# A graph network in two passes: relu rows summed in two halves of the partitions, late products of quads in pass 1

## The reference

```python
h = jnp.maximum(_layernorm(x, axis=-1), 0.0)
# layer 0
msg = jnp.concatenate([h[src], edge_attr_64], axis=-1)
messages = jax.nn.relu(msg @ W1 + b1) @ W2 + b2
aggregated = jax.ops.segment_sum(messages, dst, num_segments=6250)
g = jax.nn.relu(jnp.concatenate([h, aggregated], axis=-1) @ U1 + c1)
x = x + g @ U2 + c2
# layer 1
h = jnp.maximum(_layernorm(x, axis=-1), 0.0)
x = x + jax.ops.segment_sum(h[src] * edge_weight[:, None], dst, num_segments=6250)
```

## Time and profile before

| | |
|---|---|
| median of 3 runs | 2678.31 us (2675.13 to 2681.20) |
| the profiled execution | 2659.47 us |
| its span | 2657.7 us |
| busy in the span: TensorE, VectorE, ScalarE, GpSimd | 77%, 49%, 37%, 64% |
| DMA | 414 MB, mean 156 GB/s |
| chain that ended last | GpSimd 62%, issue 19%, TensorE 9%, DMA 8% |

### The profile page before, as it was taken

One profiled execution on the slowest core, in us unless ns is written; L12 is line 12 of the kernel. 1 busy time (PEld: TensorE's weight loads), 2 busy tenths in 40 slices (PEclk: granted clock), 3 DMA queues, 4 the chain that ended last, 5 costly groups with the idle time before them and its releaser, 6 DMA issues.

```text
span 2657.7 us, 57208 instructions
## 1 busy us (share of the span) xinstructions
PE 2049.9 (77%) x21651; PEld 1747.1 (66%) x21651; DVE 1311.2 (49%) x4334; ACT 974.0 (37%) x2419; POOL 1691.7 (64%) x1659
## 2 busy tenths in 40 slices
PE   5766666777777877777787777877778878999998
PEld 5555555656665666666666666766666767787886
DVE  6655555555555555556555555555555551111122
ACT  3334344444444444444444444444444441000111
POOL 6777777777777777777777777777777771000000
PEclk9988888888888888888888898889899899999998
DMA  3455444454444444334333333333223226999995
GB/s 88 129 169 173 162 159 159 165 171 140 142 140 148 130 132 135 118 119 127 106 109 113 99 97 94 87 94 85 74 74 82 65 62 240 401 377 384 372 350 163
DMA packets 422423, 414.27 MB, mean 156 GB/s; under 512 B 288562, under 2 KB 374178, under 8 KB 416000
## 3 DMA queue, kind: packets, MB, share of 16 engines
q1 hardware_dynamic: 369348, 354.89, 38.6%
q0 software_dynamic: 52064, 53.17, 8.8%
q10 hardware_dynamic: 732, 2.48, 0.4%
HBM read 258.64 MB, written 151.74 MB: 154 GB/s over the span
## 4 chain that ended last, share of the span: by engine, by line
POOL 62%; issue 19%; PE 9%; DMA 8%; DVE 1%; DVEq 0%; SPq 0%; ACT 0%; POOLq 0%
POOL rows L608 62%; DMA stage<-adjacency 7%; PE pair L1032 5%; PE pair L1039 1%; PE pair L1022 1%; PE pair L1045 1%; PE pair L864 1%; DMA x_all<-in_x_dram 1%; PE pair L852 0%; DVEq L1363 0%; PE pair L960 0%; PE pair L1053 0%; DVE nodes L1368 0%; DVE mean L1140 0%; SPq L490 0%
## 5 line engine op out<-in xcount | busy, mean ns | idle before, releaser
L608 POOL DMA_INDIRECT rows<-table,idx x1616 | 1649.4, 1021 | 512.0 <-issue 492.2
L721 ACT COPY stage<-pair 128x300 f32<-128x300 f32 x1616 | 622.3, 413 | 689.8 <-PE pair L946 687.3
L946 PE MATMUL pair<-bld 128*128 128x300 bf16 x4848 | 813.1, 316 | 4.5 <-DVE bld L1329 4.5
L923 PE MATMUL pair<-w1b,rings 128*128 128x128 f32 x1616 | 307.1, 349 | 530.4 <-DVE rings L1305 530.3
L923 PEld LDWEIGHTS pair<-w1b,rings 128*128 128x128 f32 x1616 | 261.2, 246 | 588.3 <-DVE rings L1305 587.9
L946 PEld LDWEIGHTS pair<-bld 128*128 128x128 bf16 x4848 | 552.2, 120 | 134.7 <-DVE bld L1329 7.9
L1329 DVE TENSOR_TENSOR bld<-bld,part 128x512 bf16<-128x512 bf16 x1212 | 432.4, 410 | 0.0
L1323 DVE TENSOR_TENSOR bld<-iota_lo,lo 128x512 bf16<-128x512 f16 x404 | 172.5, 427 | 471.1 <-PE pair L946 468.3
L1325 DVE TENSOR_SCALAR bld<-iota_key,key 128x300 bf16<-128x300 f16 x1616 | 383.5, 300 | 0.0
L1305 DVE TENSOR_TENSOR rings<-rows,pair 128x512 f32<-128x512 f32 x202 | 138.3, 685 | 461.4 <-DMA rows<-table,idx 461.4
L1032 PE MATMUL pair<-stage,h 125*64 125x96 f32 x5870 | 297.4, 253 | 25.0 <-DMA stage<-adjacency 22.2
(11 more groups left out here) (131 smaller groups left out, 779.3 us busy)
## 6 DMA issues: line engine op xcount, KB each, us to landing
stage<-adjacency SPq DMA_DIRECT2D x270, 480.0 KB, 9.4
rings<-in_edge_attr_dram SPq DMA_DIRECT2D x202, 256.0 KB
adjacency<-stage SPq DMA_DIRECT2D x28, 1200.0 KB
rows<-table,idx POOLq DMA_INDIRECT x1616
adjacency<-stage SPq DMA_DIRECT2D x20, 1080.0 KB
adjacency<-stage SPq DMA_DIRECT2D x20, 960.0 KB
adjacency<-stage SPq DMA_DIRECT2D x20, 840.0 KB
adjacency<-stage SPq DMA_DIRECT2D x20, 720.0 KB
```

The source lines that it names most:

```text
L608: pool.indirect_dma_start(out=rows[:, slot, t, :], out_offset=None, in_=table, in_offset=bass.IndirectOffsetOnAxis(ap=idx[:, g, t:t + 1], ...
L721: act.copy(tiles[:, g % STAGE, :, t * WT:(t + 1) * WT], build_bank[i % 3][:, 0:KEYS].rearrange("p (h w) -> p h w", w=WT)).then_inc(tile_ke ...
L923: last = pe.matmul(bank[:, a * P:(a + 1) * P], eaT[:, slot, a, :], w1b2[:, :], start=True, stop=True)
L946: last = pe.matmul(build_bank[i % 3][:, 0:KEYS], hot_w[q % 2][k][:, :, u], hot_key[q % 2][:, u, :], start=(k == 0), stop=(k == PARTS - 1))
```

## The change

Three things.

1. *Sums of relu rows in two halves.* sum_hid uses 64 columns of weights and puts even and odd tiles' sums in the two halves of the partitions of sum_bank; acc1 becomes sums1 on 128 partitions, met by w2u twice (w2u_twice). The count of edges now comes from hot_sum, VectorE's sum of the one-hot rows over tiles (sum_hot), by one matmul with ones; it is added to one row (96) of nodes beside hT, where u1_deg holds b2 @ U1b. sum_hid moves from between tiles 4 and 5 to behind turn_ea.
2. *Late products.* A **quad** is four groups, two batches. A chunk that gets ready after a quad's groups were stored is multiplied in pass 1 all the same: SP loads the chunk's columns of the four groups back (load_late, four pieces of 960 bytes per partition, 480 KB in all, two slots) and the quad's partial sums with them (96 KB), TensorE multiplies 5 matmuls of 192 columns (late), VectorE adds the product to the sums (keep_late), SP stores them again (store_late). At most two in a step, none in the four steps after SUMMED[c], where mid_bank is in use. The table gives 207 of them from step 29 to 201: two in each of 102 steps, one in three.
3. *Pass 2.* pieces(b) starts at multiplied(b) = ready_for(b) + late products of the quad: 9 for batches 0 to 21 and 94 to 100, 8 for 22 to 93. Every batch has a partial. put loads both starts before both adds. adjacency is one tensor, partial has the batches side by side.

There is also one more memset of 33 partitions by GpSimd at the start (the neighbours of the count's row), and small matmuls and copies for the weights.

```diff
     def ready_for(b):
-        return sum(READY[c] <= 2 * b + 2 for c in range(CHUNKS - 1))
+        first = b // 2 * 2 if b // 2 < QUADS else b
+        return sum(READY[c] <= 2 * first + 2 for c in range(CHUNKS - 1))
...
+    waiting = [(c, q) for c in range(CHUNKS - 1) for q in range(QUADS) if c >= ready_for(2 * q)]
+    for s in range(GROUPS):
+        LATE_AT[s] = []
+        if any(SUMMED[c] <= s < SUMMED[c] + GAP for c in range(CHUNKS)):
+            continue
+        while waiting and len(LATE_AT[s]) < 2:
+            c, q = waiting[0]
+            if s < max(READY[c], QUAD * q + QUAD + 3):
+                break
+            waiting.pop(0)
...
+            def load_late(n, c, q, fresh):
+                if fresh:
+                    for slot in range(STAGE):
+                        sp.wait_ge(adj_stored[slot], 16 * (q + 1))
+                wait_count(sp, late_done, n - LATE + 1)
+                sp.dma_start(late_piece[:, n % LATE, :].rearrange("p (g w) -> p g w", g=QUAD),
+                             adjacency[QUAD * q:QUAD * q + QUAD, :, c * CW:(c + 1) * CW].rearrange("g p w -> p g w")
+                             ).then_inc(late_loaded[n % LATE], 16)
...
+                    sp.dma_start(late_sum[n % BACK], sums_of(2 * q, 2)).then_inc(late_back[n % BACK], 16)
...
+            def store_late(n, q):
+                sp.wait_ge(late_kept, n + 1)
+                sp.dma_start(sums_of(2 * q, 2), late_sum[n % BACK]).then_inc(late_stored[n % BACK], 16)
...
+                    for n, c, q in LATE_AT.get(s - 1, []):
+                        store_late(n, q)
                     if SLOTS <= s + 4 < GROUPS:
                         load_ea(s + 4, s % TWO)
+                    for n, c, q in LATE_AT.get(s + 1, []):
+                        load_late(n, c, q, q not in LATE_QUAD[:n])
...
+            pool.memset(nodes[D:DEG + 1, 0:N], 0.0).then_inc(pool_step, 1)
...
-                segment(sum_bank, hid, slot, slot, D + 1).then_inc(group_done, 1)
+                for t in range(T):
+                    pe.matmul(half_of(sum_bank, t)[:, 0:W], hid[:, slot, t, 0:D], hot[:, slot, t, :],
+                              start=(t < 2), stop=(t >= T - 2))
+                wait_step(pe, hot_summed, g)
+                pe.matmul(sum_bank[D:P, W:2 * W], ones[:, 0:D], hot_sum[:, slot, :], start=True,
+                          stop=True).then_inc(group_done, 1)
...
+            def late(s):
+                for i, (n, c, q) in enumerate(LATE_AT.get(s, [])):
+                    if i == 0:
+                        wait_count(pe, late_kept, n)
+                        wait_count(pe, x1_made, sum(SUMMED[k] < s for k in range(CHUNKS)))
+                    pe.wait_ge(h2_staged, c + 1)
+                    pe.wait_ge(late_loaded[n % LATE], 16 * (n // LATE + 1))
+                    held = late_piece[0:NP, n % LATE, :].rearrange("p (g h c) -> p g h c", g=QUAD, c=GC)
+                    for h in range(BLK):
+                        last = pe.matmul(half_of(mid_bank, h)[:, i * QCOLS:(i + 1) * QCOLS],
+                                         h2[:, (c * BLK + h) * D:(c * BLK + h + 1) * D], held[:, :, h, :],
+                                         start=(h < 2), stop=(h >= BLK - 2))
+                    last.then_inc(late_done, 1)
...
+            def sum_hot(g):
+                wait_step(dve, hot_made, g)
+                dve.tensor_reduce(hot_sum[:, g % TWO, :], hot[:, g % TWO, :, :].rearrange("p t w -> p w t"), AX_X,
+                                  ALU.add).then_inc(hot_summed, 1)
...
+            def keep_late(s):
+                products = LATE_AT.get(s, [])
+                if products:
+                    dve.wait_ge(late_done, products[-1][0] + 1)
...
+                        dve.tensor_tensor(to, of, to, ALU.add).then_inc(late_kept, 1)
...
             def put(b):
+                starts = [dve.value_load(base_row[0:1, 2 * b + o:2 * b + o + 1], min_val=0, max_val=N)
+                          for o in range(2)]
+                dve.wait_ge(f_made, b + 1)
                 for o in range(2):
-                    start = dve.value_load(base_row[0:1, 2 * b + o:2 * b + o + 1], min_val=0, max_val=N)
-                    to = acc2[:, ds(start, W)]
-                    if o == 0:
-                        dve.wait_ge(f_made, b + 1)
+                    to = acc2[:, ds(starts[o], W)]
                     wait_count(dve, acc2_added, 2 * b + o)
                     dve.tensor_tensor(to, to, add_bank[:, o * W:(o + 1) * W], ALU.add).then_inc(acc2_added, 1)
```

137 lines of the change are left out of this document (104 added, 33 removed).

## The result

The changed kernel takes **2601.11 us** (median of 4 runs, 2595.76 to 2607.44), the kernel before, timed beside it, 2676.72 (4 runs). The ratio is 0.9719, 95% interval 0.9694 to 0.9744: faster by 76 us, as to the sign what was forecast, and half of the 150 us; the time lies over the range's 2590.

What follows compares the result with a forecast made beforehand. Gathers were taken to set pass 1's pace and loads to hold pass 2. Costs of 3 + 5 + 5 us and minus 163 in pass 2 gave minus 150, hence 2528 us, range 2485 to 2590.

Steps and rivals of the forecast that it cites:

- 62 batches with ten products: Pass 2, up to batch 83: 2.4 us a batch (bounds 2.01 and 2.46), 149 us in all.
- the clock falls in pass 2: Rival, chance 0.11: TensorE at half clock in pass 2, ten-product batches 3.85 us; in all 72, 104 us more, 2632.
- 22 five-product batches: Pass 2: 2.91 us each, the earlier trace's rate at half clock, 64 us in all.
- the case in which half of the batches are slow: Pass 2, within the rival of the falling clock: half of the 72 ten-product batches at 3.85 us, 2580 us.
- The bounds: Pass 2's minus 163 us lay between minus 190 and minus 150; the cheaper rival (0.18) was 2492, the range's low end 2485.
- Late products: Pass 1, TensorE: 0.96 us for each late product, 1.9 us a step with two (bounds 0.94 and 3.2), hidden under the gathers.
- TensorE full: Rival, chance 0.11: halves don't overlap in pass 1, late products take 3.2 us a step, 51 us over the gathers, 2574.
- late loads: Rival, chance 0.05: pass 1's loads for late products land late, 147 to 252 us paid, about 2775 at the latter.
- VectorE: Pass 1: 1.4 us more a late step, 0.49 of it the new reduce; 7.3 of 10.6 us, hidden.
- Gathers: Pass 1: GpSimd's gathers slowed by VectorE's new work, 5 us taken, between 0 and 22; by the skill's rule 0.
- Startup: Start of the kernel: one more GpSimd memset holds up VectorE's mean, 3 us taken (0 to 5.3).
- TensorE's idle before L1024: Sign that the forecast is right: this idle time falls below half of the kernel before's, there at L923.

Runs made afterwards that it cites:

- burst22: The changed kernel with 20 dummy matmuls put once in TensorE's queue ahead of batch 22's products, the first batch with ten: 2557.11 us in one run.
- the two half-changes: The changed kernel with only the sums in halves (no late products), and with only the late products (sums as before): 2681.54 and 2613.82 us.
- late_alone_c: The changed kernel with its late products but the sums as before the change: 2613.82 us, ratio 0.9757 to the kernel before.

## Why the prediction was wrong

- **The step that failed is the rate of the "62 batches with ten products"**, 2.4 us "the clock left aside", and with it the 0.11 given to the rival *the clock falls in pass 2*. That rival is what happened, in all 72 batches. I had read batches 84 to 93 at full clock as evidence against it. They came behind batches of more products each, at DMA share 1.04 and 92 of 100 us of TensorE: they kept a clock, they did not have to raise it. Earlier in the same trace the clock did fall and rise, behind a wait for pieces:

```profile
2445.74 1.05 PE L1032 MATMUL pair<-stage,h 125*64 125x96 f32 x20 [2.47 <-DMA stage<-adjacency]
2446.99 1.87 PE L1032 MATMUL pair<-stage,h 125*64 125x96 f32 x20 [0.20 <-DMA stage<-adjacency]
...
2450.54 4.70 PE L1032 MATMUL pair<-stage,h 125*64 125x96 f32 x70
...
2456.20 3.19 PE L1032 MATMUL pair<-stage,h 125*64 125x96 f32 x70
```

  There it came back in the midst of a batch of 35 products, 7 us after it had fallen; batches of ten never brought it back by themselves. In the changed kernel the ten-product batches come behind a stretch with 7 of 26 us idle and 22 five-product batches, for which I had myself taken the half clock of the earlier trace rows. Having written 2.91 us for those, I should have asked what brings the clock up again. burst22 shows that something must: at half clock the ten-product batches stay there.
- The Trainium skill (TensorE: Matmul & The Clock Gate, its table of states) has the clock return to the full rate once TensorE has been busy for a while; the windows with 100.00 of 100.00 us busy at 0.50, and 363.6 us without a return, disagree, if busy in the profile is what the page means by it. Its section on HAM oscillation has the clock going down and up between groups; here it did so in pass 1 and up to 2244.1 us, then fell and stayed, so the case in which half of the batches are slow did not occur. What the prediction cites on micro-idling stands on that page in its section on a second HAM failure mode.
- The rival's own price was too high. It had 2.91 + 0.94 = 3.85 us; at half clock five products more take 1.87 - 1.22 = 0.65, so 2.91 + 0.65 = 3.56, measured 3.55, and 83 + 7 us instead of 104. With that the rival's time would have been 2528 + 90 = 2618, and less the 13 us that pass 1 and the start did not cost, 2605: measured 2601. That it comes so near is in part luck, since single executions differ by more.
- The 22 five-product batches at 2.91 us: right to the digit.
- put: 2.4 us with an upper bound of 2.46 for loads that don't overlap. They don't: 2.47. The sum had stayed just under that bound; at full clock it would have been 72 x 0.07 = 5 us short.
- The bounds were not added up from their terms. At 2.01 and 2.27 us a batch pass 2 would win 205 us, not 190, and at 2.46 it would win 158, not 150; and 2492 less 72 x 0.26 is 2473, not 2485. The measured time lies on the other side.
- *Late products*: two take 2.1 us of a step (forecast 1.9, from 0.32 us a matmul, which stands in no row), TensorE waits 0.5 us for their loads in all, and with 344 of 400 us busy its cover held where the gathers set the pace. The rivals *TensorE full* and *late loads* did not occur there. That on three chips the same change slows the kernel is a case that no row of the profile before could show.
- *VectorE*: the reduce took 0.774 us, not 0.49. I had priced it by the number of elements read, from a reduce to 5 columns; this one writes 40 per partition and reads across tiles, and which of the two costs the time no run shows. Hidden all the same: 275 of 400 us.
- *Gathers* 5 us: 1028 ns against 1021 would be 11 us, but the means of kernels with the same pass 1 go from 1026 to 1032, of the two half-changes to 1036 and 1037, and the medians leave no room for more than a few us. The 1036 is that of late_alone_c, which has no reduce at all, so nothing here speaks against the 0 that the prediction worked out by the Trainium skill (SBUF — State Buffer; the sentence on tensor_reduce stands in its section on who interferes with whom). Not settled in size.
- *Startup* 3 us: the first gather starts at 65.4 where it started at 63.3, 2.1 us.
- Of what was to show it: gathers on "issue" only, 101 pieces, the last gather within 15 us of 2204 (2218.6) came; TensorE's idle before L1024 was to fall below half of today's and is 465 us, against 530 for L923: the sums' matmuls fell from 280 us busy (L929) to 135 (L1039) and the clock of the late steps rose from 0.91 to 0.94, which gave back part of the 221 us that the late products (L1081) took. That sign was badly chosen. The ten-product batches and the clock of 0.5 were named as the sign of the clock rival, and are what was seen.

## What to carry to other kernels

When an edit thins the work of a stage, work out TensorE's rate for it at both clock levels and ask which level the stage is entered at, not only whether it would hold the upper one: the same batches ran at 2.47 or 3.55 us, and one unneeded matmul per batch was worth 79 us. Moving work into an earlier stage to shorten a later one pays only down to the point where the later one's next limit stands; here leaving more chunks in 84 batches was 76 us faster, and what stood in the way was the clock: with a dummy in every batch the full move did as well (2523 against 2525 us), and with the shorter ring besides it took 2479. A cost that lies under a cover (here the gathers') should be stated with the cover: on chips where the gathers wait for VectorE instead, the same change cost 3.6%.

## What the runs showed of the hardware that was not expected

- The clock has two lasting levels under the same ten-product batches: 1.00 with TensorE busy 92.3 of 110 us held for 119.5 us and then fell; 0.50 with TensorE busy 100.00 of 100 us did not rise in 363 us (363 to 366 us in the other traces with the late products and no dummy). With one matmul more per batch it rose from 0.50 and held for 191 us (97.6 of 110 us busy).
- A load of a start into a VectorE register costs some 0.6 us in VectorE's queue, two in a row 1.18, not less; taken ahead of a wait they are hidden (a batch of 2.14 us instead of 2.47).
- Two reduces of 320 elements per partition differ by a half: 0.49 us to 5 columns, 0.774 to 40 with a stride.
- One program, the kernel before: 2668 to 2678 us on the chips of the first kind, 3370 to 3452 on three others. There the changed kernel's trace has TensorE's weight loads waiting on "issue" for up to 11.6 us in pass 1, while in pass 2 a batch takes the same 3.55 or 2.14 us to the hundredth.
